# A decoder layer on one Trainium2 core: attended outputs in the banks of the turned probabilities, and three steps moved in their engines' order

## What is computed

```python
x = x + attn(layernorm(x))         # softmax over positions of x @ W_A, as 16 Toeplitz matrices, times x @ W_V, then W_O, + b_O
x = x + xattn(layernorm(x), ctx)   # causal attention: Q from x, K and V from ctx, one head of 256
x = x + ffn(layernorm(x))          # 2 shared experts + 16 routed ones, top 2, silu(g) * u, then down
...
# routing
probs = softmax(flat @ router_w)
weights, indices = top_k(probs, 2)
weights = weights / (weights.sum() + 1e-9)
comb = sum(one_hot(indices) * weights)
...
h = silu(g) * u * comb
```

## Time and profile before

| | us |
|---|---|
| runs | 660.12, 662.44, 662.88; median 662.44 |
| profiled execution, its own time | 663.9 |
| its span, first to last instruction | 662.1 |
| PE, DVE busy in it | 579.7 (88%), 470.4 (71%) |
| ACT, POOL busy in it | 224.6 (34%), 193.6 (29%) |
| mean granted clock of TensorE | 0.970 |
| maximum of z (L951) starts in iterations 0 to 7 | 20.5, 48.6, 110.5, 184.6, 258.7, 328.3, 397.7, 467.0 |
| Toeplitz products of iteration 8 start | 535.0 |
| down product of the last pair ends | 657.4 |

### The profile page before, as it was taken

How to read it: one execution, slowest core, us unless ns; L and a number is a source line. 1 busy time by engine, 2 the same in 40 slices (tenths; PEclk the granted TensorE clock), 3 DMA queues, 4 the chain that set the end, 5 groups by cost and what they waited for, 6 DMA issues and landing times. The chain is left out here.

```text
span 662.1 us, 13826 instructions
## 1 busy us (share of the span) xinstructions
PE 579.7 (88%) x5212; PEld 385.3 (58%) x5212; DVE 470.4 (71%) x1137; ACT 224.6 (34%) x450; POOL 193.6 (29%) x221
## 2 busy tenths in 40 slices
PE   2687697999999999999998999899989979997596
PEld 1365366655675557555775567556755656564254
DVE  4585476777877598868886888778876757677243
ACT  3554243433333323333333333333333222422121
POOL 4406121242333133312233322323232212232122
PEclk9889599999999999999999999999999999999789
DMA  7885724591119611591139012931184115000500
GB/s 255 308 278 177 240 105 183 112 335 67 64 38 267 212 64 34 123 295 34 63 77 310 29 63 63 285 100 63 39 226 156 65 34 129 1 1 33 130 0 33
DMA packets 61249, 84.26 MB, mean 127 GB/s; under 512 B 2832, under 2 KB 46736, under 8 KB 60944
## 3 DMA queue, kind: packets, MB, share of 16 engines
q1 hardware_dynamic: 61200, 83.60, 41.9%
HBM read 71.47 MB, written 12.12 MB: 126 GB/s over the span
## 5 line engine op out<-in xcount | busy, mean ns | idle before, releaser
L536 POOL TENSOR_TENSOR mid<-gated,mid 128x512 f16<-128x512 f32 x80 | 93.3, 1167 | 257.6 <-ACT mid L681 257.6
L877 DVE SCALAR_TENSOR_TENSOR gated<-gated,score 128x512 f32<-128x512 f32 x80 | 54.3, 679 | 53.0 <-ACT gated L676 53.0
L140 PE MATMUL wide<-w_d,mid 128*128 128x256 f16 x320 | 87.4, 273 | 3.6 <-POOL mid L536 3.5
L681 ACT ACTIVATE mid<-gated 128x512 f16<-128x512 f32 x80 | 50.1, 626 | 112.0 <-DVEq L889 111.7
L142 PE MATMUL wide<-w_d,mid 128*128 128x256 f16 x320 | 87.2, 273 | 0.0
L141 PE MATMUL wide<-w_d,mid 128*128 128x256 f16 x320 | 87.2, 273 | 0.0
L140 PE MATMUL score<-h3T,w_gu 128*128 128x512 f16 x160 | 62.1, 388 | 6.8 <-DVEq L120 5.3
L676 ACT ACTIVATE gated<-score 128x512 f32<-128x512 f32 x80 | 47.2, 590 | 59.8 <-PE score L142 56.4
L140 PE MATMUL rows<-h3T,w_gu 128*128 128x512 f16 x160 | 61.2, 383 | 6.4 <-DVE gated L886 5.2
L141 PE MATMUL score<-h3T,w_gu 128*128 128x512 f16 x160 | 62.2, 389 | 0.0
L142 PE MATMUL score<-h3T,w_gu 128*128 128x512 f16 x160 | 62.1, 388 | 0.0
(11 more groups left out here) (193 smaller groups left out, 1369.3 us busy)
## 6 DMA issues: line engine op xcount, KB each, us to landing
toep<-z_scratch SPq DMA_DIRECT2D x16, 2048.0 KB, 16.1
stage<-comb_scratch SPq DMA_DIRECT2D x32, 512.0 KB, 7.7
x_in<-in_x SPq DMA_DIRECT2D x8, 512.0 KB, 11.5
out<-x_out SPq DMA_DIRECT2D x8, 512.0 KB, 3.0
qT<-q_scratch SPq DMA_DIRECT2D x7, 512.0 KB, 3.7
vx<-v_scratch SPq DMA_DIRECT2D x7, 512.0 KB, 4.9
q_scratch<-stage SPq DMA_DIRECT2D x6, 512.0 KB, 5.9
v_scratch<-stage SPq DMA_DIRECT2D x6, 512.0 KB, 6.6
```

The source lines that it names most:

```text
L140: pe.matmul(out, stationary[0], moving[0], start=start, stop=False, **kw)
L536: pool.tensor_tensor(mid[:, 1, j % SLOTS], gated[:, j % SLOTS], mid[:, 0, j % SLOTS], ALU.subtract).then_inc(mid_split.sem, 1)
L681: act.activation(mid[:, 0, j % SLOTS], gated[:, j % SLOTS], ACT.Copy).then_inc(mid_hi.sem, 1)
L877: dve.scalar_tensor_tensor(to, to, 1.0, score.bank(f"g{j}")[:], ALU.add, ALU.mult).then_inc(score.taken.sem, 1)
```

## The change

The attended outputs `p0` to `p3` leave the `rows` banks and go into the `turned` banks, among the turned probabilities. In `rows` the up products then alternate between the two banks. PE turns the probabilities of a block before it makes the attended output of the block before, and DVE takes them in the same order. On DVE `route` goes ahead of z's maximum, z's reciprocal behind `weigh`; on ACT the router's two exponentials go ahead of z's. POOL adds the bias after the low half of pair 1. `gate` is cut into `open_gate` (L877, L883) and `pass_gate` (L886), and for pair 2 the second goes behind the low halves of `h2T`.

```diff
-TURNED = ["mix.0", "mix.1", "combT", "h2.0", "h2.1", "pt0", "pt1", "pt2", "pt3", "h3.0", "h3.1", "h1.0", "h1.1", "none"]
+TURNED = ["mix.0", "mix.1", "combT", "h2.0", "h2.1", "pt0", "pt1", "p0", "pt2", "p1", "pt3", "p2", "p3", "h3.0", "h3.1",
+          "h1.0", "h1.1", "none"]
...
-ROWS = (["logit", "v0", "v2", "u0", "o0", "o2", "u1", "u2", "u3", "u4", "p0", "u5", "p1", "u6", "p2", "u7"]
-        + ["p3", "u8", "u9", "none"])
+ROWS = ["logit", "v0", "v2", "u0", "o0", "o2", "u1", "u2", "u3", "u4", "u5", "u6", "u7", "u8", "u9", "none"]
...
# SP, fetch_context
-                sp.wait_ge(rows.ready.sem, rows.is_ready(it, "p3"))
+                sp.wait_ge(turned.ready.sem, turned.is_ready(it, "p3"))
...
# POOL, iteration
-                if f and m:
-
+                if first:
                     pool.wait_ge(rows.taken.sem, rows.is_taken(it, "o2"))
                     add_bias(it)
                 for j in range(MID):
                     if d and j:
                         part_mid(it - 2, j)
+                    if f and m and d and j == 1:
+                        pool.wait_ge(rows.taken.sem, rows.is_taken(it, "o2"))
+                        add_bias(it)
...
# DVE, iteration
+                if d:
+                    route(it, it - 2)
                 if f:
                     score.take(dve, it, "z")
...
                 if d:
                     weigh(it - 2)
+                if f:
+                    dve.wait_ge(z_exped.sem, z_exped.at(it, 1))
+                    dve.reciprocal(z_rsum[:], z_sum[:]).then_inc(score.taken.sem, 1)
...
                 if d:
-                    gate(it, it - 2, 2)
+                    open_gate(it, it - 2, 2)
                 if m:
                     part_turned(it, it - 1, h2T, h2T_hi, "h2")
+                if d:
+                    pass_gate(it, it - 2, 2)
...
# DVE, in the loop over j
-                        if not d and at < C:
+                        if at < C:
                             part_prob(it, it - 1, at)
                         if 0 <= at - 1 < C:
                             attended(it, at - 1)
...
-                        if d and at < C:
-                            part_prob(it, it - 1, at)
...
# PE, in the loop over j
                         at = j - AHEAD
+                        if at < C:
+                            turn_probs(it, it - 1, at)
                         if d and 0 <= at - 1 < C:
                             attend(it, at - 1)
-                        if at < C:
-                            turn_probs(it, it - 1, at)
```

More of the change, by code:

```diff
@@ L689, in iteration @@
                     part_weights(range(12, len(pieces)))
+                if d:
+                    act.wait_ge(shifted.sem, shifted.at(it - 2, 2))
+                    act.activation(e2[:], e2_in[:], ACT.Exp).then_inc(l_exped.sem, 1)
+                    act.activation(l_exp[:], l_shift[:], ACT.Exp).then_inc(l_exped.sem, 1)
                 if f:
@@ L698, in iteration @@
                     take_mix(it - 1, 0)
-                if d:
-                    act.wait_ge(shifted.sem, shifted.at(it - 2, 2))
-                    act.activation(e2[:], e2_in[:], ACT.Exp).then_inc(l_exped.sem, 1)
-                    act.activation(l_exp[:], l_shift[:], ACT.Exp).then_inc(l_exped.sem, 1)
-                if m:
                     take_mix(it - 1, 1)
@@ L862, in attended, with open_gate @@
             def attended(it, c):
-                rows.take(dve, it, f"p{c}")
+                turned.take(dve, it, f"p{c}")
                 dve.wait_ge(score.taken.sem, score.is_taken(it, f"s{c}"))
-                dve.wait_ge(rows.ready.sem, rows.is_ready(it, f"p{c}"))
-                dve.scalar_tensor_tensor(x_res[:, c], rows.bank(f"p{c}")[:, 0:E], s_rsum[:, c:c + 1], x_res[:, c],
-                                         ALU.mult, ALU.add).then_inc(rows.taken.sem, 1)
-            def gate(it, b, j):
+                dve.wait_ge(turned.ready.sem, turned.is_ready(it, f"p{c}"))
+                dve.scalar_tensor_tensor(x_res[:, c], turned.bank(f"p{c}")[:, 0:E], s_rsum[:, c:c + 1], x_res[:, c],
+                                         ALU.mult, ALU.add).then_inc(turned.taken.sem, 1)
+            def open_gate(it, b, j):
                 to = gated[:, j % SLOTS]
@@ L883, in gate, with pass_gate @@
                     dve.tensor_tensor(to, to, comb_rows[:, j - NSH], ALU.mult).then_inc(opened.sem, 1)
+            def pass_gate(it, b, j):
+                to = gated[:, j % SLOTS]
+                if j >= NSH:
                     dve.wait_ge(opened.sem, opened.at(b, j - NSH + 1))
@@ L889, in gate @@
                 dve.sem_inc(gated_done.sem, 1)
+            def gate(it, b, j):
+                open_gate(it, b, j)
+                pass_gate(it, b, j)
             def route(it, b):
@@ L955, in iteration @@
                 if d:
-                    route(it, it - 2)
                     if not m:
@@ L960, in iteration @@
                         rows.take(dve, it, "u0")
-                if f:
-                    dve.wait_ge(z_exped.sem, z_exped.at(it, 1))
-                    dve.reciprocal(z_rsum[:], z_sum[:]).then_inc(score.taken.sem, 1)
                 if d and not m:
@@ L1009, in iteration @@
                 if d:
-                    gate(it, it - 2, 2)
+                    open_gate(it, it - 2, 2)
                 if m:
                     part_turned(it, it - 1, h2T, h2T_hi, "h2")
+                if d:
+                    pass_gate(it, it - 2, 2)
+                if m:
                     for k in range(2):
@@ L1026, in iteration @@
                         if 0 <= at - 2 < C - 1:
-                            hold(dve, rows.taken, rows.is_taken(it, f"p{at - 2}"))
+                            hold(dve, turned.taken, turned.is_taken(it, f"p{at - 2}"))
                             statistics(2, x_res, [at - 2])
-                        if d and at < C:
-                            part_prob(it, it - 1, at)
                         if j - 1 < C:
@@ L1034, in iteration @@
                         if at == C:
-                            hold(dve, rows.taken, rows.is_taken(it, "p3"))
+                            hold(dve, turned.taken, turned.is_taken(it, "p3"))
                             aggregate(it - 1, 2, statistics(2, x_res, [C - 1]))
@@ L1158, in attend @@
             def attend(it, c):
-                rows.fill(pe, it, f"p{c}")
+                turned.fill(pe, it, f"p{c}")
                 pe.wait_ge(turned.taken.sem, turned.is_taken(it, f"pt{c}"))
                 for t in range(c + 1):
-                    last = three_passes(pe, rows.bank(f"p{c}")[:, 0:E], parts(probT, c % 2, slice(P * t, P * t + P)),
+                    last = three_passes(pe, turned.bank(f"p{c}")[:, 0:E], parts(probT, c % 2, slice(P * t, P * t + P)),
                                         parts(vx, t, slice(None)), start=(t == 0), stop=(t == c))
-                last.then_inc(rows.ready.sem, 1)
+                last.then_inc(turned.ready.sem, 1)
             def gate_up(it, j):
```

## The result

| | before | changed |
|---|---|---|
| runs beside each other, median (lowest to highest) | 661.28 (659.0 to 662.88) | 645.04 (644.11 to 646.66) |
| ratio, 95% interval | | 0.9752 (0.9729 to 0.9776) |
| profiled execution, its span | 662.1 | 644.9 |

The kernel is 16.2 us faster by the medians; 15.1 were forecast (a time of 647.3). The profiled span is 17.2 shorter, which has to be split up before it is laid beside the sum.

What follows compares the result with a forecast made beforehand. PE (88% busy) bounds it up to the scores, with 22.9 us of waits removable; DVE from j = 3 on. Router 4.5 + bias and h2 9.2 + attended outputs 1.4 = 15.1 off 663.9: 648.8, median 647.3; range 641 to 656.

Steps and rivals of the forecast that it cites:

- (a): PE's turning of the routing weights waits for the mix's low half, 5.8 us; gain 4.5, at most 5.0.
- The rival that ACT was late already: The mix's low half was late for ACT's sake, so its wait stays: 651.8; chance 0.06.
- (b): PE's turning of `h2` waits for DVE's `h2`, 14.3 us, 2.8 without the start's; this wait was to go.
- (c): First scores wait for `h2T`'s low half, 9.1 us in seven; with the `h2` wait, 9.2 gained.
- The up factor behind the low halves: Pair 2's up factor, 0.85 us on DVE, goes behind `h2T`, covered by PE's scores; 0.8 in iteration 8.
- After the change every iteration looks like iteration 8 here: -0.64: DVE's `h2` operations, freed of the additions beside them, fall from 2.86 to 2.22 us in every iteration.
- The price of L884 beside the additions: Pair 2's multiplication on DVE (L883 before) loses 0.3 us to part of one addition; ends 0 and all four.
- The rival that it waits for all four: The additions hold pair 2's multiplication for all four, gaining 0.2 an iteration, not 1.4: 654.5; chance 0.12.
- (d): Up products wait for DVE to take the one before, 5.2 us in seven; 1.4 gained, iterations 7 and 8 only.
- the swap keeps the counts and sums: 0: Swapping the order of `pt` and `p` on PE and DVE gains nothing, 0.
- The rival that it pays everywhere: The second up bank gains all 5.2 and its overlaps, 3.8 more: 643.5; chance 0.13.
- The slower rival: `turned` pair becomes a chain: PE stands a whole DVE gate at block 3's turning and attended 2; 671.8; chance 0.05.

Runs made afterwards that it cites:

- e1_router: Kernel before with only the router's part: route and its exponentials ahead of z's, z's reciprocal behind `weigh`; 655.26 us, ratio 0.9884.
- e8_early3: Changed kernel with bias additions earlier: three ahead of `var_eps`, last behind pair 1; in iterations 2, 3 all before pair 0's low half; 640.42 us, 0.9658 to before.
- e9_early4: Changed kernel with all four bias additions ahead of `var_eps` in iterations 4 to 7, in 2 and 3 before pair 0's low half; 641.71 us, 0.968 to before.

## Why the prediction was right, and where it was not

**The total.** 15.1 forecast, 16.2 measured, from terms of which one was far too large and two too small. All the places that the prediction named did gain, but that the total came so near is luck: errors of 3.8 one way and 4.2 the other cancelled. What follows is by stretch of PE.

**Router and z (a): right.** 4.5 forecast; Toeplitz to combT is 5.9 shorter over iterations 2 to 7 (5.6 in `e1_router` alone). The 5.0 of the waits understated it: a matmul that doesn't wait also starts 0.14 ahead of its predecessor's end, which makes 0.8 in six. L826 (L825 before) starts 7.17 behind the first Toeplitz product, from 8.17: 1.00 earlier, where 0.92 was forecast. ACT is now what it waits for, as foreseen. The rival that ACT was late already is refuted. DVE of the changed kernel, iteration 6, from a multiplication of `weigh` on:

```profile
394.33 0.29 DVE L936 TENSOR_SCALAR comb<-expert_no,top_f,w 128x16 f32<-128x16 f32 x1
...
395.59 0.14 DVE L980 RECIPROCAL z_rsum<-z_sum 16x1 f32<-16x1 f32 x1
397.98 0.69 DVE L826 SCALAR_TENSOR_TENSOR val<-rows,val 128x512 f16<-128x512 f32 x1 [2.25 <-ACT val L642]
```

**Bias and h2 (b, c): the size was off, and the sign of one step.** 9.2 forecast; combT to scores is 5.4 shorter over seven iterations. The up factor behind the low halves gave 1.0 an iteration, 6.8 in seven by itself, where 0.85 was taken: right in kind, and low. The step that failed reads "After the change every iteration looks like iteration 8 here: -0.64". Iteration 8 has nothing behind pair 1's low half. In the others the additions come right behind it and still meet the last operation of `h2`: -0.23 in iterations 4 to 6, and +0.1 to +0.2 in 2, 3 and 7. "(b) goes" failed with it: PE's six waits for `h2` are 2.6, from 2.8. DVE and POOL of the changed kernel, iteration 6, against the earlier trace rows:

```profile
409.25 2.63 DVE L809 TENSOR_SCALAR h<-x_res,mean_var,rstd 128x256 f32<-128x256 f32 x4 [0.30 <-POOL rstd L531]
...
412.61 1.09 DVE L884 TENSOR_TENSOR gated<-gated,stage 128x512 f32<-128x512 f32 x1
413.62 1.27 DVE L819 TENSOR_TENSOR h2T<-turned,h2T 128x512 f16<-128x512 f32 x2
```

```profile
410.96 3.32 POOL L543 TENSOR_TENSOR x_bo<-x_in,b_o 128x256 f32<-128x256 f32 x4
```

In iteration 7 they meet two, and `h` takes 3.04, more than the 2.93 it took before. The price of L884 beside the additions was put at 0.3 and is 0.25 over the 0.84 or 0.94 of before, 0.4 to 0.5 over 0.69: that was about right. The rival that it waits for all four is refuted in iterations 4 to 6. The third addition, L884 and the fourth addition of iteration 6:

```profile
412.43 0.72 POOL L543 TENSOR_TENSOR x_bo<-x_in,b_o 128x256 f32<-128x256 f32 x1
412.61 1.09 DVE L884 TENSOR_TENSOR gated<-gated,stage 128x512 f32<-128x512 f32 x1
413.11 1.17 POOL L543 TENSOR_TENSOR x_bo<-x_in,b_o 128x256 f32<-128x256 f32 x1
```

L884 starts while the third one runs (to 413.15) and is done at 413.70; the fourth, until 414.28, is the one that becomes long. In iterations 2, 3 and 7 L884 meets the last of the four, so there the two mechanisms can't be told apart, and it takes 1.19. But with only 0.23 won on `h2`, and only in three iterations, and that price paid, the move is worth less than nothing: +1.3 in the stretches it touches, alone and in the changed kernel (+1.28 and +0.98 over iterations 2 to 7). Of the 11.9 of waits in (b) and (c) 6.8 are left (2.6 and 4.2), 1.0 an iteration, where 0.4 was forecast.

The low half of `h2T`, which reads PSUM, kept its 1.27 although its first operation lies beside the last addition, which ends at 414.28; the prediction had no row for that. By the Trainium skill, page "SBUF — State Buffer", section "Who interferes with whom", a DVE instruction with at most one SBUF input, outside the two-port modes, doesn't contend with GpSimd. The trace agrees here.

**Attended outputs (d): too low.** 1.4 forecast (1.4 for `u6`'s two waits, 0 for the swap); scores to h3 is 4.2 shorter: 0.44 to 0.50 in each of iterations 2 to 6 and 0.91 in 7 and 8. That DVE sets the pace was right, and for that reason the swap counted: it shortened the stretch by 0.3 to 0.5 an iteration, in iterations 4 to 6 by the pauses that it took out of DVE, which "the swap keeps the counts and sums: 0" passed over. The bank gave 0.53 in each of iterations 7 and 8, where 0.7 was forecast, and 0.17 in three others, where it was 0. The rival that it pays everywhere is refuted as a mechanism, though 5.2 was nearer to the part's total.

**The slower rival.** PE waits for the probabilities three times, 1.0 us in all, and for no attended output. The waits are 0.26 to 0.49 long, once in each of iterations 4 to 6, where PE turns block 3, the place that the prediction named. The pauses that the rival needed, of a whole gate each, don't occur.

**The sum.** The term of bias and `h2` came out 3.8 smaller; the banks gave 2.8 more and the router 1.4 more over iterations 2 to 7, and Toeplitz to combT of iteration 8, for which nothing was forecast, became 0.4 longer. Start and end of the kernel made +2.3 and -4.1 of the profiled difference. What part of these two is due to the change wasn't separated; the start varies by as much between the twelve kernels (44.7 to 47.9), and the end lies between 58.9 (changed) and 63.1 (before) but is 61.8 in `e8_early3`, which does the same as the changed kernel there.

## What to carry over

When a block of work is moved away from an operation that it obstructs, lay its new start and end against every exposed operation near the new place and against the old one, and don't take an iteration that lacks the block as the model. An engine that sets the pace profits from a mere swap if the pauses between its own operations differ, so count pauses as well as operations. Which of an edit's several moves pays is settled by making each alone, and read from stretches of the trace rather than from medians when the clock's level shifts the total by more than the part is worth.

## What the runs showed of the hardware

Operations of 128x16 on DVE, 0.28 us alone, took 1.28 and 1.01 beside a POOL operation, and ended within 0.1 us of its end. A DVE multiplication with both inputs in SBUF took 0.69 alone, 0.84 or 0.94 when it began 0.3 or 0.4 before the end of a POOL operation, and 1.09 to 1.20 when it began within one of four additions that follow each other. In iteration 6 of the changed kernel it was done 0.55 after the end of the addition that ran when it began, and one more addition was still to come: between POOL operations that follow each other DVE got its turn.

The price is mutual. In the changed kernel's iteration 6 the addition that began while L884 was under way (413.11) took 1.17, and the one before it 0.72, so the four took 3.32. In iterations 2, 3 and 7, where L884 begins in the last of them and none follows, the four take 2.93, as they did beside `h2` in the kernel before. In `e9_early4`, where they lie beside neither, they take 2.78.

DVE stood 0.25 us between a gate's last operation and one that adds a PSUM product to SBUF with a per-partition scale (L867), and 0.15 before the one that makes the probabilities' low half from PSUM (L859). Why they differ wasn't tried.

The lower level of the clock came at different places around iteration 9 in kernels with the same work there. The last 50 to 30 us of the kernel before and of the changed one (granted clock 0.76 and 0.91; the two windows don't hold quite the same matmuls):

```profile
612.00:632.00 20.00, 13.10 (x53) 5.52 (x51) 6.30 (x10) 3.62 (x6) 3.46 (x3) 0.76 0.47 108
```

```profile
595.00:615.00 20.00, 12.72 (x65) 6.75 (x64) 8.44 (x19) 3.19 (x6) 2.77 (x4) 0.91 0.50 107
```

In them the first matmul of iteration 9's first gate product, 128x512, took 0.61 in the kernel before (at 1.2 GHz), behind an idle time of 5.29, and 0.39 in the changed one (at 2.4 GHz), behind one of 3.50:

```profile
623.39 0.61 PE L140 MATMUL score<-h3T,w_gu 128*128 128x512 f16 x1 [5.29 <-DVEq L120]
```

```profile
609.84 0.39 PE L140 MATMUL score<-h3T,w_gu 128*128 128x512 f16 x1 [3.50 <-DVEq L120]
```

In `e8_early3` the first five matmuls of that product took 0.38 or 0.39, and the first matmul of the next product, behind a second idle time of 1.47, took 0.61: the clock had fallen although PE had resumed.

```profile
602.67 0.39 PE L140 MATMUL score<-h3T,w_gu 128*128 128x512 f16 x1 [3.77 <-DVEq L120]
605.71 0.61 PE L140 MATMUL score<-h3T,w_gu 128*128 128x512 f16 x1 [1.47 <-DVE gated L887]
```
